# Attention inside a transformer tower on one core: the vector engine masks a tile before it takes the next tile's maximum

## The reference, cut to what matters

```python
W = jnp.einsum('bqd,bkd->bqk', Q, K) / scale
tril = jnp.tril(jnp.ones((S_len, S_len), dtype=W.dtype))
M = jnp.where(W == 0, jnp.zeros_like(W), tril[None, :, :])
x_max = jnp.max(W, axis=-1, keepdims=True)
x_exp = jnp.exp(W - x_max) * M
A = x_exp / (jnp.sum(x_exp, axis=-1, keepdims=True) + EPS)
return jnp.einsum('bqk,bkd->bqd', A, V)
```

## Time and profile before

| | |
|---|---|
| median of 3 runs | 421.12 us (418.02 to 422.26) |
| profiled execution, its own time | 418.62 us |
| span of its trace | 416.8 us |
| PE busy | 371.0 us (89%) |
| DVE busy | 274.4 us (66%) |
| ACT busy | 200.9 us (48%) |
| POOL busy | 116.8 us (28%) |
| attention, first `score(2)` to the end of the last mask | about 42 to 287 us |
| experts' part | about 290 us to the end |

### The profile page before, as it was taken

How to read it: one execution, slowest core, us unless ns; L and a number is a source line. 1 busy time by engine, 2 the same in 40 slices (tenths; PEclk the granted TensorE clock), 3 DMA queues, 4 the chain that set the end, 5 groups by cost and what they waited for, 6 DMA issues and landing times. The chain is left out here.

```text
span 416.8 us, 8088 instructions
## 1 busy us (share of the span) xinstructions
PE 371.0 (89%) x2716; PEld 175.0 (42%) x2716; DVE 274.4 (66%) x582; ACT 200.9 (48%) x387; POOL 116.8 (28%) x197
## 2 busy tenths in 40 slices
PE   5887899999999999999999967857978999999985
PEld 3554244445345444434435434424456433333332
DVE  3132667777877977967967978797334365655665
ACT  0233255455555546546546555456714565556521
POOL 4050202415414414324325324226300730000000
PEclk9989699999999999999999999999958999999999
DMA  6989901801800900900000000000000010011112
GB/s 150 221 156 221 171 2 40 165 0 39 165 2 17 186 0 1 200 0 0 0 0 2 2 1 0 2 1 2 2 0 0 3 27 16 12 26 27 27 27 50
DMA packets 29085, 20.42 MB, mean 49 GB/s; under 512 B 12376, under 2 KB 28928, under 8 KB 29056
## 3 DMA queue, kind: packets, MB, share of 16 engines
q1 hardware_dynamic: 28448, 19.91, 23.7%
q10 hardware_dynamic: 608, 0.12, 0.2%
HBM read 17.93 MB, written 2.10 MB: 48 GB/s over the span
## 5 line engine op out<-in xcount | busy, mean ns | idle before, releaser
L777 DVE TENSOR_REDUCE rmax<-Sp 128x1 f32<-128x1024 f32 x64 | 78.2, 1222 | 27.4 <-PE Sp L1135 26.7
L1135 PE MATMUL Sp<-eT,G 64*64 64x512 f32 x512 | 70.6, 620 | 22.3 <-issue 18.1
L503 ACT ACTIVATE PT<-PTp 128x512 f32<-128x512 f32 (+2 forms) x96 | 43.5, 489 | 48.4 <-PE PTp L1150 48.2
L402 POOL TENSOR_SCALAR_AFFINE_SELECT EP<-EP 128x128 f32<-128x128 f32 x64 | 23.0, 360 | 149.1 <-ACT EP L556 149.1
L556 ACT ACTIVATE EP<-Sp,negm 128x128 f32<-128x128 f32 (+3 forms) x64 | 47.7, 745 | 24.0 <-DVE negm L779 23.5
L787 DVE SCALAR_TENSOR_TENSOR EP<-Sp,EP 128x128 f32<-128x128 f32 (+3 forms) x64 | 48.1, 751 | 15.4 <-PE PTp L1150 9.4
L1150 PEld LDWEIGHTS PTp<-ident,EP 128*128 128x128 f32 x288 | 31.8, 143 | 43.9 <-issue 36.9
L1150 PE MATMUL PTp<-ident,EP 128*128 128x128 f32 x288 | 45.3, 285 | 3.5 <-DVE EP L787 2.8
L1135 PEld LDWEIGHTS Sp<-eT,G 64*64 64x64 f32 x512 | 14.9, 132 | 49.6 <-issue 49.6
L1168 PE MATMUL MM<-PT,e 128*64 128x512 f32 (+1 forms) x192 | 34.2, 491 | 0.5 <-ACT PT L503 0.3
L979 DVE SCALAR_TENSOR_TENSOR PT<-PTp,negc,XW 128x512 f32<-128x512 f32 x30 | 21.1, 746 | 18.1 <-PE PTp L1305 12.3
(11 more groups left out here) (264 smaller groups left out, 585.8 us busy)
## 6 DMA issues: line engine op xcount, KB each, us to landing
XW<-in_x_dram SPq DMA_DIRECT2D x6, 1024.0 KB, 10.0
X<-in_x_dram SPq DMA_DIRECT2D x6, 1024.0 KB, 10.8
out_dram<-xc SPq DMA_DIRECT2D x16, 128.0 KB, 2.0
XW<-in_x_dram SPq DMA_DIRECT2D x2, 576.0 KB, 8.8
X<-in_x_dram SPq DMA_DIRECT2D x2, 576.0 KB, 14.2
XW<-in_x_dram SPq DMA_DIRECT2D x2, 448.0 KB, 11.7
X<-in_x_dram SPq DMA_DIRECT2D x2, 448.0 KB, 13.7
EP<-in_L_tok_W_dram SPq DMA_DIRECT2D x2, 144.0 KB, 3.2
```

Source lines behind the costliest of these rows:

```text
L402: pool.affine_select(out=blk_, in_=blk_, compare_op=ALU.is_ge, fill=0.0, base=0, pattern=[[-1, 128]], channel_multiplier=1).then_inc(tri_d ...
L503: return act.activation(dst, src, ACT.Copy)
L777: dve.reduce_max(rmax[:, t:t + 1], Sp[t % 2][:, :], AX).then_inc(max_done, 1)
L1135: ins = pe.matmul(Sp[t % 2][64 * s:64 * s + 64, CH * c:CH * c + CH], G[q][rows, 128 * t + 64 * s:128 * t + 64 * s + 64], eT[q][rows, :], **ON)
```

## The change

In the loop over the tiles on DVE, `mask(b, q, t)` is moved in front of `smax(b, q, t + 1)`. At t = 7 the order was that already and stays.

```diff
@@ -879,10 +879,10 @@
 
             def body(b, q, first=False, last=False):
                 for t in range(NT):
+                    mask(b, q, t)
                     if t < NT - 1:
                         smax(b, q, t + 1)
-                    mask(b, q, t)
-                    if t == NT - 1 and not last:
+                    elif not last:
                         smax(b + 1, 1 - q, 0)
                     if not last:
                         if t == 0:
```

## The result

| | before | changed |
|---|---|---|
| median | 420.94 us (418.02 to 422.26, 4 runs) | 430.82 us (429.05 to 431.74, 4 runs) |
| ratio | | 1.0226, 95% interval 1.0176 to 1.0276 |
| profiled execution, span | 418.62, 416.8 us | 431.74, 429.5 us |
| its mean granted clock | 0.969 | 0.959 |

What follows compares the result with a forecast made beforehand. PE was taken to bound the looped batches, a loop of waits batches 6 and 7. Terms: -0.3 + 1.7 + 4 x 1.2 + 3.9 = +10.1 us, giving 428.7 or 431.2; it took 430.0 us, range 421.5 to 436.

Steps and rivals of the forecast that it cites:

- The bound: PE bounds the looped batches, idle only 0.7 to 1.9 us each; in the last two windows a loop of waits does.
- ACT's list at tile 6: At t = 5, expo(6) 1.86 us later delays class_exp and the U copies, so PE stands 1.0 us before o_group.
- The empty gain at score(2): Next batch's head: the 0.53 us stall before score(2) goes, but u_group still waits for copies behind z_turn.
- The contention of L753: L753 beside POOL's feature sum drops from 1.15 to 0.5 to 0.7 us; a batch costs 1.2, by the row alone 1.7.
- A looped batch: Sum for one looped batch: 1.0 - 0.2 + 0.3 + 0.1 = +1.2 us, bounds +0.4 and +1.7.
- batch 0: Earlier mask(0) up to mask(5) gives -0.3 us; from there to batch 1 a larger o_group stall costs +1.7.
- Batches 6 and 7: Last two batches, where the new loop is longer: 0.5 + 2.1 + 1.6 = +4.2 us, taken as 3.9, bounds +2 and +5.5.
- Tile 6 to 7: In batches 6 and 7, mask(6) to mask(7) grows by 1.0 us, from 3.27 to 4.28.
- Tile 5 to 6: In batches 6 and 7, tile 6 costs +0.9 us: exponential 0.54, and class_exp and p0_rest 0.3.
- the credit at the batch's head: In batches 6 and 7, tile 0 gives -0.2 us: one maximum and the shortest exponential replace two maxima in a row.
- The sign of 32 us for batch 6: Expected in the changed kernel's trace: the last two batches take 32 and 29 us; wrong if not above 30.3 and 27.7.
- The clock: Rival, chance 0.07: TensorE's granted clock falls to half over batch 7, costing +4 us, so 434 us.

Runs made afterwards that it cites:

- The dose: Every exponential written twice, in the old order and in the new order: 438.1 us (ratio 1.040) and 471.7 us (1.120) against the kernel before.
- tile 0: Mask first at t = 0 alone, old order for all other tiles, against the kernel before: 425.5 us, ratio 0.999.
- tile 5 alone: Mask first at t = 5 only, old order for all other tiles, against the kernel before: 432.6 us, ratio 1.023.
- tiles 0 to 3: Mask first at t = 0 to 3, old order at t = 4 to 6, against the kernel before: 428.1 us, ratio 1.012.
- old in 6, 7: New order in batches 0 to 5 only, old order in the last two batches: 428.9 us, ratio 1.019 to the kernel before.
- class first: The changed kernel with class_exp alone put ahead of expo on ACT at t = 1 and t = 5: 427.0 us, ratio 1.013 to the kernel before.

## Why the prediction was right, point by point

- **The bound.** Right: PE in the looped batches, the loop in batches 6 and 7. The dose showed the second.
- **ACT's list at tile 6.** Right in every link. Forecast 1.86 us later for expo(6) and 1.0 us of standing PE; measured 2.39 - 0.61 = 1.78 and 0.74. About half of that difference is o_group's start, 4.52 us behind the start of mask(5) instead of the 4.69 forecast: expo(6) came 0.08 us earlier, the U copies started 0.10 behind class_exp instead of 0.13, and o_group 0.04 behind their end instead of 0.10. The rest is PE, which came free 3.78 us behind the start of mask(5) instead of 3.66. mask(6) came 4.22 us behind mask(5), forecast 4.4, before 4.48.
- **The empty gain at score(2).** Right, and shown by tile 0.
- **The contention of L753.** Forecast 0.5 to 0.7 us, measured 0.54. The Trainium skill (SBUF — State Buffer, on the engine ports) describes the exclusive port pair; that the line ended with POOL's sum in both traces agrees. A batch cost 0.9 us and not the 1.7 of the row alone; what the shorter line is worth in it was not tested by itself.
- **A looped batch.** Forecast +1.2, measured +0.88. The sum counts four such and batch 0 (+1.7 and -0.3) and has 6.2; of the fifth looped batch it takes only 0.5, in the term for batches 6 and 7. That is 6.7 forecast for batches 0 to 5. Measured are 4.4 for the five and 1.2 - 0.4 for batch 0, together 5.2.
- **Batches 6 and 7.** The direction was right, the size of the sum was not. Tile 6 to 7 was forecast at +1.0 and measured at +0.97 in batch 6. Tile 5 to 6 was +0.9 and came to +0.39: this step took 3.84 us before, where the loop of 2.64 and a mask of 0.96 make 3.60; p0_rest stood between the masks then too. And the credit at the batch's head was taken as 0.2: step 0-1 gained 1.07 us and step 7-0 0.43 in batch 6. In the old order DVE waited there for z_turn's copy (0.57 us) and for L753 (1.17); in the new one maximum 1 fills the wait, and L753 takes 0.54. So batch 6 cost 0.3 us instead of 2.1, and batch 7 about 2.2 instead of 1.6: 2.5 us instead of 3.7, or of the 3.4 that the sum kept of it. The sign of 32 us for batch 6 came true (31.85) only with 1.3 us of low clock in it.
- **The clock.** This was a rival with a chance of 0.07 and a price of 4 us. It happened, beside the forecast rather than in its place, and cost some 2.9 us in the profiled execution, which had the longest time of the four.
- **Luck in the total.** By its own terms the forecast has 10.1 us, and the order cost 7.7 in the two traces. The medians differ by 9.9. So the hit to within 1 us rests in part on the clock, which added about what the sum had too much; in the two traces another 2.0 us lie ahead of the first maximum. How these parts divide in the executions without a trace is not shown.

The version that beats both kernels is mask first at tiles 0 to 4: ratios of 0.995 (0.991 to 0.999) and 0.993 (0.989 to 0.997) in two series. The clock has a share in that, but not the whole: at a mean clock of 0.965 to 0.966 the kernel before took 420.3 to 421.3 us and this one 417.8 to 419.3. It keeps the early mask where exponentials are short, and leaves maximum 6 ahead of mask(5) and maximum 7 ahead of mask(6).

## What to carry to other kernels

An order of two instructions on one engine decides which of two latencies is hidden: here the score on PE or the exponential on ACT and its triangle on POOL. Before swapping, add up both for every tile size, and then follow the late result through the in-order list of its engine, to small steps queued behind it that someone else waits for. And cut the trace into stages with the granted clock beside each, since two orders with equal looped batches differed by 9 us behind them: 2.4 us by the order, most of the rest in stretches of low clock. Mixing the two orders has a price of its own, too: where a tile with the mask first is followed by one in the old order, two maxima stand between two masks (step 5-6 of batch 6 with tile 5 alone, 5.62 us against 3.84).

## What the runs showed of the hardware

With tiles 0 to 3, a pause of PE of 2.17 us in batch 6 was followed 0.6 us later by 7 us at 1.2 GHz; with tiles 0 to 4, the same place with a pause of 1.15 us was not. The pause's length is not the whole of it: one of 1.76 us in the same batch saw the clock fall in one trace (old in 6, 7) and not in another (before), and 2.50 us did not lower it in a third (class first). The total of one kernel then moves by 5 to 7 us without any change in its work: the kernel before measured 418.0 us at a mean clock of 0.969 and 423 to 425 at 0.953.

An instruction of VectorE beside one of GpSimd took 1.15, 0.54 or 0.17 us by when it started: where L753 met the sum on POOL it ended 0.02 to 0.04 us behind it, in batches 2 to 6 of both traces (138.77 and 138.73 before, 143.85 and 143.82 changed), and it took 0.17 where POOL's sum was not there.
